# A scan and mixture-of-experts kernel: state handed over by GpSimd, C rows spread for two steps at a time, float32r weight parts used from the third tile on

## The chip, the cores and the metric

The kernel runs on one core of a Trainium2 chip. The metric is the device time of one execution in microseconds (us). The core has five engines with queues of their own that run in program order: TensorE (PE, matmul; its weight loads are shown as PEld), VectorE (DVE), ScalarE (ACT), GpSimd (POOL) and SyncE (SP, which issues the DMAs here). Semaphores order them against each other.

## The reference, cut to what matters

Per batch b (4 of them, 256 positions, width 256) a state-space layer is computed and then a feed-forward layer with two shared and eight routed experts:

```python
delta = softplus(dt_proj(dt_lo) + b);  A = -exp(A_log)          # 256 channels, 16 states
def step(state, (d_t, B_t, C_t, u_t)):
    state = state * exp(d_t[..., None] * A) + (d_t * u_t)[..., None] * B_t[:, None, :]
    return state, einsum('ben,bn->be', state, C_t)
y = (scan of step over 256 positions + D*u) * silu(z);   x = x + tanh(g0) * y
h = silu(x' @ Wg_e.T) * (x' @ Wu_e.T) for 2 shared + 8 experts (x' = layernorm(x)), FF = 176
out = x + tanh(g1) * (shared_down + 2.5 * top-2 weighted expert_down)
```

## The kernel before, in words

**Scan.** The 256 channels are two halves of 128 partitions. A *step* m takes two of the 16 states (NS = 2) over one half of the positions (128 of 256), for both channel halves: a tile of 128 x 512 in four rows of 128 columns. A batch has 16 steps: 0 to 7 of it do the first half of the positions, 8 to 15 the second, so there are 64 steps and 8 half-batches, called *tiles* (numbers 0 to 7). For a step ScalarE writes the decays exp(delta*A) into PSUM (`exps`, L642, four activations, ring psA of two); GpSimd writes delta*u*B (`times_b`, L1010, ring dbu of three); VectorE scans (L896, L902) and multiplies with C (`prod`, L913, ring of three); GpSimd adds the products of the steps of a tile (L1034; for tile 0 TensorE does, L528). C comes from TensorE, which spreads a row of C over the 128 partitions by a matmul with a 0/1 matrix `sel` (`spread_c`, L518, one step at a time, ring psC of two).

The first-half steps scan all four rows with one instruction: column 0 of each row of the decays is zero, so a row starts afresh. ScalarE keeps the last column of each row (`keep_ends`, L721, `ends`). The second-half steps need four instructions of 128 columns, each with its `ends` column as initial value (L902), and their decays have 128 columns instead of 127. Before the next batch ScalarE zeroes column 0 again (L638).

**From scan to experts.** When GpSimd has added the eight products of a tile (`prod` i on GpSimd is the addition of step i; the last ones are 15, 23, 31 ...), TensorE sums it with D*u (`y_sum`, L541, L545), VectorE gates (`gate_y`), TensorE transposes, VectorE adds the residual and the statistics, GpSimd makes the variance (`variance`, L1061 to L1067, four small operations), ScalarE normalizes, and the tile goes through ten *units* (units 10t to 10t+9): `up` on TensorE, `gate` on ScalarE (L771) and VectorE (L984), `mul` on VectorE (L807, L811). A unit with even j is two float32 matmuls (L599, each two instructions in the trace). One with odd j is six float32r matmuls (L609 to L611) on the high and low parts of weights and features (`whi`, `wlo`, `hnhi`, `hnlo`); the parts of the weights are made once, early, by ScalarE (`weights_hi`, L763) and GpSimd (`weights_lo`, L1054) from a staged copy that lies in `hcat`; unit 1 waits for all five. Four groups of a tile's hidden columns are transposed (L583), copied (`hidden`, L780) and multiplied with the down weights (`down`, L451, all 28 instructions of a tile at one place), accumulated in psD, which `y_sum`, `to_tokens`, `to_features` and `logits` use too. Then `finish` (L991) and the output DMA.

**Order.** Every engine follows a list of tasks written out by hand (`ORDER`, L88), `task:number`. A GpSimd or ScalarE task `scan:i` prepares step i+1. Start: `z_stats:0` to `z_stats:3` on VectorE need the input x (the last three batches by `d_x`), then `split0:0` to `split2:0`, `log_1:0`, `log_2:0`, `delta0:0` to `delta2:0`, and after that the first `dbu`. SP sends at the start ctx, w_x, w_dt, sel (768 KB), ident and x, then after the first projection B (broadcast), `staged` (two DMAs of 880 KB), `wup` (two of 880 KB) and `wdn`.

## Time and profile before

| what | value |
|---|---|
| median of 3 runs (lowest to highest) | 270.29 us (270.20 to 270.37) |
| the profiled execution's own time | 269.66 us |
| its span, first to last instruction | 267.7 us |
| mean granted TensorE clock (share of full) | 0.923 |
| PE busy, share of the span | 222.0 us, 83% |
| PEld busy | 167.9 us, 63% |
| DVE busy | 227.0 us, 85% |
| ACT busy | 175.5 us, 66% |
| POOL busy | 182.0 us, 68% |
| chain that ended last | PE 40%, DVE 24%, POOL 22%, issue 7%, DMA 3% |

The span is the time between the first and the last instruction that the profiler saw; the execution's own time is 1.96 us longer. Busy shares are means over stages with different limits; the profile also tells of each engine's idle time what ended it.

### The profile page before, as it was taken

The numbers are of one execution on the slowest core, as the hardware profiler recorded it, in microseconds if no ns is written. First come the engines' busy times: TensorE is split into PE (matmuls) and PEld (weight loads), VectorE is DVE, ScalarE is ACT, GpSimd is POOL, SyncE is SP. The second block draws the span as 40 slices with busy tenths as digits, with TensorE's granted clock in tenths as the row PEclk, the third lists the DMA queues.
The fourth block names the chain that finished last, engine by engine and source line by source line (L and its number), as shares of the span: only waits on it lengthen the run. The fifth ranks groups of instructions, "written<-read, shape, count | busy, mean of one in ns | idle before, by whom it ended". The sixth has DMA issues, their size and how long they took to land.

```text
span 267.7 us, 4168 instructions
## 1 busy us (share of the span) xinstructions
PE 222.0 (83%) x1093; PEld 167.9 (63%) x1093; DVE 227.0 (85%) x590; ACT 175.5 (66%) x536; POOL 182.0 (68%) x187
## 2 busy tenths in 40 slices
PE   8841983576847589999968979999999989999994
PEld 3421652354625368778746767687787778678883
DVE  1789999999999999999999998999798999563231
ACT  3579989965799695857577886584674562251121
POOL 0238999999899999998574998989586574120000
PEclk9985698559997599999999997999999999999999
DMA  6789953000025000000071000000000000000000
GB/s 175 230 269 386 364 189 157 0 0 2 0 80 240 0 1 0 22 1 0 24 271 44 1 20 2 2 0 22 0 1 21 2 0 0 20 2 1 21 0 20
DMA packets 9559, 17.34 MB, mean 65 GB/s; under 512 B 824, under 2 KB 8800, under 8 KB 8928
## 3 DMA queue, kind: packets, MB, share of 16 engines
q1 hardware_dynamic: 9248, 16.94, 18.3%
q8 instruction: 8, 0.13, 0.2%
q10 hardware_dynamic: 288, 0.16, 0.2%
q14 instruction: 15, 0.12, 0.1%
HBM read 15.97 MB, written 1.11 MB: 64 GB/s over the span
## 4 chain that ended last, share of the span: by engine, by line
PE 40%; DVE 24%; POOL 22%; issue 7%; DMA 3%; ACT 2%; SPq 1%; DVEq 0%; POOLq 0%; ACTq 0%
PE psD L451 14%; PE psU L599 11%; POOL dbu L1010 11%; DVE hs L902 7%; POOL acc L1034 5%; POOL wlo L1054 3%; PE psM L583 3%; DVE ag L984 3%; DVE prod L913 3%; PE psU L609 3%; DMA x_sb<-in_x 3%; PE psU L610 3%; PE psU L611 3%; DVE hs L896 3%; DVE hcat L811 2%
## 5 line engine op out<-in xcount | busy, mean ns | idle before, releaser
L1010 POOL TENSOR_TENSOR dbu<-du,bb 128x512 f32<-128x512 f32 x64 | 80.5, 1273 | 9.9 <-DVE du L379 4.6
L642 ACT ACTIVATE psA<-delta,aneg 128x127 f32<-128x127 f32 (+1 forms) x256 | 78.2, 357 | 6.2 <-DVE hs L902 3.4
L1034 POOL TENSOR_TENSOR acc<-acc,prod 128x512 f32<-128x512 f32 x42 | 54.2, 1291 | 16.4 <-DVE prod L913 15.0
L599 PE MATMUL psU<-wup,hnT 128*128 128x352 f32 x160 | 58.9, 493 | 1.7 <-DVE hcat L807 1.0
L771 ACT ACTIVATE tg<-psU 128x176 f32<-128x176 f32 x80 | 24.7, 315 | 48.3 <-PE psU L599 29.4
L902 DVE TENSOR_TENSOR_SCAN hs<-psA,ends,dbu 128x128 f32<-128x128 f32 x128 | 50.4, 456 | 0.2 <-DVE prod L913 0.2
L451 PE MATMUL psD<-wdn,hT 128*128 128x256 f32 x224 | 50.2, 380 | 0.0
L451 PEld LDWEIGHTS psD<-wdn,hT 128*128 128x128 f32 x224 | 42.1, 190 | 5.8 <-DVE wtok L977 0.3
L913 DVE TENSOR_TENSOR prod<-hs,psC 128x512 f32<-128x512 f32 x64 | 41.9, 673 | 0.6 <-DVE hs L896 0.4
L984 DVE SCALAR_TENSOR_TENSOR ag<-tg,psU 128x176 f32<-128x176 f32 x80 | 25.3, 327 | 17.8 <-ACT tg L771 17.5
L896 DVE TENSOR_TENSOR_SCAN hs<-psA,dbu 128x512 f32<-128x512 f32 x32 | 38.3, 1209 | 0.3 <-POOL dbu L1010 0.3
L599 PEld LDWEIGHTS psU<-wup,hnT 128*128 128x128 f32 x160 | 28.9, 199 | 13.4 <-DVE hcat L811 2.1
L609 PE MATMUL psU<-whi,hnhi 128*128 128x352 f32 x80 | 32.5, 406 | 1.4 <-DVE hcat L811 1.3
L518 PE MATMUL psC<-parts,sel 96*128 96x128 bf16 x128 | 16.7, 236 | 13.2 <-DVE prod L913 12.8
L610 PE MATMUL psU<-wlo,hnhi 128*128 128x352 f32 x80 | 26.3, 328 | 0.0
L611 PE MATMUL psU<-whi,hnlo 128*128 128x352 f32 x80 | 26.2, 327 | 0.0
L811 DVE SCALAR_TENSOR_TENSOR hcat<-psU,wtok,ag 128x176 f32<-128x176 f32 x64 | 24.4, 394 | 1.0
L518 PEld LDWEIGHTS psC<-parts,sel 96*128 96x128 bf16 x128 | 10.5, 107 | 22.7 <-DVE prod L913 15.9
L780 ACT COPY hT<-psM 128x512 f32<-128x512 f32 (+1 forms) x32 | 16.1, 502 | 13.2 <-PE psM L583 13.0
L583 PE MATMUL psM<-ident,hcat 128*128 128x128 f32 x112 | 18.0, 277 | 4.0 <-DVE hcat L811 3.8
L609 PEld LDWEIGHTS psU<-whi,hnhi 128*128 128x128 f32 x80 | 15.8, 197 | 4.8 <-DVE hcat L811 3.4
L583 PEld LDWEIGHTS psM<-ident,hcat 128*128 128x128 f32 x112 | 12.4, 140 | 8.9 <-issue 4.5
(117 smaller groups left out, 317.3 us busy)
## 6 DMA issues: line engine op xcount, KB each, us to landing
bb<-brows SPq DMA_DIRECT2D x3, 2048.0 KB, 7.1
hcat<-in_w_up SPq DMA_DIRECT2D x2, 880.0 KB, 8.9
wup<-in_w_up SPq DMA_DIRECT2D x2, 880.0 KB, 11.6
wdn<-in_w_down SPq DMA_DIRECT2D x1, 1664.0 KB, 14.1
x_sb<-in_x SPq DMA_DIRECT2D x4, 256.0 KB, 6.8
bb<-brows SPq DMA_DIRECT2D x1, 1024.0 KB, 4.7
out<-outb SPq DMA_DIRECT2D x8, 128.0 KB, 1.7
sel<-in_sel SPq DMA_DIRECT2D x1, 768.0 KB, 6.0
```

What stands on the lines that cost most here:

```text
L451: last = pe.matmul(psD[:, :], hT[0:m, g % HT_RING, c:c + P], wdn[0:m, f, :], start=(f == 0), stop=(f == FB - 1))
L583: last = pe.transpose(psM[0:m, c:c + P], hcat[:, t % 2, f * P:f * P + m], ident[:, :])
L599: last = pe.matmul(dst, hnT[:, b % 2, k, lh * P:(lh + 1) * P], wup[:, j // 2, k, :], start=(k == 0), stop=(k == KT - 1))
L609: pe.matmul(dst, h_hi, w_hi, start=(k == 0), stop=False)
L610: pe.matmul(dst, h_hi, w_lo, start=False, stop=False)
L611: last = pe.matmul(dst, h_lo, w_hi, start=False, stop=(k == KT - 1))
L642: last = act.activation(dst[:, j, h, c:], delta[:, b % 2, h, l0 + c:l1], ACT.Exp, scale=aneg[:, h * DS + s0 + j:h * DS + s0 + j + 1])
L896: dve.tensor_tensor_scan(hs[:, i % 2], psA[:, i % DA_RING], dbu[:, i % DBU_RING], 0.0, ALU.mult, ALU.add).then_inc(s_scan, 1)
L902: last = dve.tensor_tensor_scan(hs[:, i % 2, row], psA[:, i % DA_RING, row], dbu[:, i % DBU_RING, row], ends[:, i % HALF, c:c + 1], ALU.mu ...
L913: dve.tensor_tensor(tile(prod[:, i % PROD_RING]), tile(hs[:, i % 2]), c.unsqueeze(2).broadcast_to([P, NS, EH, l1 - l0]), ALU.mult).then_in ...
L1010: pool.tensor_tensor(tile(dbu[:, m % DBU_RING]), du[:, b % 2, :, l0:l1].unsqueeze(1).broadcast_to(shape), bb[:, b % 2, s0:s0 + NS, l0:l1]. ...
L1034: pool.tensor_tensor(acc[:, p % 2], before, prod[:, i % PROD_RING], ALU.add).then_inc(s_add, 1)
```

## The change

1. **Hand-over of the state.** The second half is scanned with one instruction of 512 columns too. ScalarE makes the decays of position 128 for a whole batch (`decay`, two activations of 16 columns, four times). GpSimd multiplies them with `ends`, four steps at a time (`carry`, 128 x 16, eight times), and adds the result into column 0 of the four rows of `dbu` (`fix`, 128 x 4, 32 times). VectorE's second-half scan waits for its `fix`. The zeroing copies (L638) are gone, all decays have 127 columns.
2. **C rows.** `spread_c:i` does steps 2i and 2i+1 and waits for the products up to 2i-3; ring psC is still two of 512 columns, so it holds four steps. `sel` is 96 x 32 instead of 96 x 32 x 128, and read with a step of 0.
3. **Weights.** All ten raw units lie in `wup`, loaded by two DMAs of five whole units each. Units j = 1, 5, 9 use float32r parts from tile 2 on and j = 3, 7 from tile 3 on; before that they are float32 (12 of 80 units change). `weights_lo` waits for its own unit; four are made where five were, the fifth behind step 36's dbu. `features_hi` and `features_lo` of tiles 0 and 1 go.
4. **Down.** Transposing, copying and the down product are tasks of one group each (`turn`, `hidden`, `down`, 32 of each).
5. **All lists are written anew**, SP's too (`finish:1` now behind `xproj:3 dt:3`). VectorE's begins `z_stats:0 z_stats:1 split0:0 split1:0 split2:0 z_stats:2 z_stats:3 log_1:0`; GpSimd has `z_stats:3` at the start.

`step_range`, `sum_of` and `tiles_in` also know an unhalved batch, but `HALVED` is true for all four, so the steps are those of before.

```diff
+SPLIT = ((1, 2), (3, 3), (5, 2), (7, 3), (9, 2))
+CONVERT = sorted(range(NSPLIT), key=lambda k: (SPLIT[k][1], SPLIT[k][0]))
...
     "SyncE": """
-        xproj:0 dt:0 xproj:1 dt:1 xproj:2 dt:2 finish:0 finish:1 xproj:3 dt:3 finish:2 finish:3 finish:4
+        xproj:0 dt:0 xproj:1 dt:1 xproj:2 dt:2 finish:0 xproj:3 dt:3 finish:1 finish:2 finish:3 finish:4
...
     "GpSimd": """
+        z_stats:0 z_stats:1 z_stats:2 z_stats:3 first:0 scan:0 scan:1 scan:2 scan:3 scan:4 weights_lo:0 scan:5
+        scan:6 carry:0 weights_lo:1 scan:7 scan:8 scan:9 fix:8 fix:9 fix:10 weights_lo:2 weights_lo:3 carry:1
+        scan:10 scan:11 fix:11 prod:9 fix:12 scan:12 scan:13 fix:13 fix:14 prod:10 variance:0 delta0:1 scan:14
...
-        sel = sb("sel", [P, 2 * DS, P], BF16)
+        sel = sb("sel", [P, 2 * DS], BF16)
...
-                        for k in range(KT):
-                            sp.dma_start(staged[:, :, k], w_up[:, 1::2, k]).then_inc(d_wst, 16)
-                        for k in range(KT):
-                            sp.dma_start(wup[:, :, k], w_up[:, 0::2, k]).then_inc(d_wup, 16)
+                        for k in range(2):
+                            sp.dma_start(wup[:, NU // 2 * k:NU // 2 * (k + 1)],
+                                         w_up[:, NU // 2 * k:NU // 2 * (k + 1)]).then_inc(d_wup[k], 16)
...
                     if i >= 2:
-                        pe.wait_ge(s_prod, i - 1)
-                    for j in range(NS):
-                        last = pe.matmul(psC[:, i % 2, j * P:(j + 1) * P], sel[0:XROWS, DS + s0 + j, :],
-                                         parts[:, b % 2, l0:l1], start=True, stop=True)
+                        pe.wait_ge(s_prod, 2 * i - 2)
+                    for m in (2 * i, 2 * i + 1):
+                        b, s0, ns, l0, l1 = step_range(m)
+                        for j in range(ns):
+                            c = m % 2 * L + j * (l1 - l0)
+                            last = pe.matmul(psC[:, i % 2, c:c + l1 - l0], row(DS + s0 + j),
+                                             parts[:, b % 2, l0:l1], start=True, stop=True)
...
+                    if j not in SLOT or t < SPLIT[SLOT[j]][1]:
+                        for k in range(KT):
+                            last = pe.matmul(dst, hnT[:, b % 2, k, lh * P:(lh + 1) * P], wup[:, j, k, :],
+                                             start=(k == 0), stop=(k == KT - 1))
+                    else:
+                        slot = SLOT[j]
+                        if t == SPLIT[slot][1]:
+                            pe.wait_ge(s_wlo, CONVERT.index(slot) + 1)
...
-                if m % DS in (0, 1) and m >= DS:
-                    act.copy(dst[:, :, :, 0], tile(zeros[:, 0:NS * EH])[:, :, :, 0])
-                c = 1 if l0 == 0 else 0
...
+                elif task == "decay":
+                    act.wait_ge(s_delta, i + 1)
+                    for h in range(EH):
+                        last = act.activation(dec[:, i % 2, :, h], aneg[:, h * DS:(h + 1) * DS], ACT.Exp,
+                                              scale=delta[:, i % 2, h, P:P + 1])
+                    last.then_inc(s_dec, 1)
...
-                    if l0 == 0:
-                        dve.tensor_tensor_scan(hs[:, i % 2], psA[:, i % DA_RING], dbu[:, i % DBU_RING], 0.0,
-                                               ALU.mult, ALU.add).then_inc(s_scan, 1)
-                    else:
-                        dve.wait_ge(s_ends, ends_of(i))
-                        for c in range(NS * EH):
-                            row = slice(c * P, (c + 1) * P)
-                            last = dve.tensor_tensor_scan(hs[:, i % 2, row], psA[:, i % DA_RING, row],
-                                                          dbu[:, i % DBU_RING, row], ends[:, i % HALF, c:c + 1],
-                                                          ALU.mult, ALU.add)
-                        last.then_inc(s_scan, 1)
+                    if second_half(i):
+                        dve.wait_ge(s_fix, ends_of(i))
+                    dve.tensor_tensor_scan(hs[:, i % 2], psA[:, i % DA_RING], dbu[:, i % DBU_RING], 0.0,
+                                           ALU.mult, ALU.add).then_inc(s_scan, 1)
...
+                elif task == "carry":
+                    b, j = divmod(i, 2)
+                    k0, k1 = j * HALF // 2, (j + 1) * HALF // 2
+                    pool.wait_ge(s_ends, HALF * b + k1)
+                    pool.wait_ge(s_dec, b + 1)
...
+                elif task == "fix":
+                    heads = dbu[:, i % DBU_RING].rearrange("p (c l) -> p c l", l=P)[:, :, 0]
+                    pool.wait_ge(s_dbu, i + 1)
+                    pool.wait_ge(s_carry, 2 * (i // DS) + (1 if i % HALF < HALF // 2 else 2))
+                    pool.tensor_tensor(heads, heads, carry[:, i % HALF], ALU.add).then_inc(s_fix, 1)
```

## Rows read from the trace of the kernel before

**Rows 1.** Busy time by stretch: PE, PEld, DVE, ACT, POOL, PEclk, DMA share, GB/s
```profile
55.00:90.00 35.00, 22.90 (x105) 16.29 (x104) 34.24 (x89) 27.57 (x96) 33.44 (x31) 0.84 0.16 62
90.00:114.50 24.50, 23.52 (x119) 18.24 (x120) 23.85 (x67) 17.74 (x53) 23.75 (x24) 0.94 0.02 6
114.50:146.60 32.10, 29.10 (x156) 23.02 (x156) 31.64 (x79) 22.63 (x76) 22.68 (x25) 1.00 0.19 71
146.60:227.90 81.30, 77.90 (x404) 61.54 (x403) 75.28 (x203) 51.86 (x167) 62.25 (x60) 0.98 0.02 6
227.90:265.00 37.10, 35.66 (x179) 28.41 (x177) 15.14 (x51) 10.76 (x31) 2.10 (x6) 1.00 0.02 8
```

**Rows 2.** Timeline, start: start us, us, engine, line, op, shapes, count [idle before]
```profile
11.69 0.41 ACT L682 CAST parts<-xdbl 96x256 bf16<-96x256 f32 x1
...
12.15 0.75 DVE L921 BATCH_NORM_STATS2 zst<-x_sb 128x6 f32<-128x256 f32 x2 [1.19 <-DMA x_sb<-in_x]
...
13.10 0.72 DVE L921 BATCH_NORM_STATS2 zst<-x_sb 128x6 f32<-128x256 f32 x2
...
14.65 0.58 ACT L699 ACTIVATE psC<-psC 128x512 f32<-128x512 f32 x1
...
16.17 0.67 DVE L875 TENSOR_SCALAR dy<-psC 128x512 f32<-128x512 f32 x1
```

**Rows 3.** Groups by line on DVE: count, busy us, mean ns, idle before
```profile
L902 DVE TENSOR_TENSOR_SCAN hs<-psA,ends,dbu 128x128 f32<-128x128 f32 x128 | 50.4, 456 | 0.2 <-DVE prod L913 0.2
...
L896 DVE TENSOR_TENSOR_SCAN hs<-psA,dbu 128x512 f32<-128x512 f32 x32 | 38.3, 1209 | 0.3 <-POOL dbu L1010 0.3
```

**Rows 4.** Groups by line on POOL
```profile
L1010 POOL TENSOR_TENSOR dbu<-du,bb 128x512 f32<-128x512 f32 x64 | 80.5, 1273 | 9.9 <-DVE du L379 4.6 <-DVE hs L902 3.4 <-DVE hs L896 1.7
...
L1050 POOL TENSOR_TENSOR hnlo<-hnT,hnhi 128x256 fp32r<-128x256 f32 x8 | 5.8, 728 | 3.4 <-ACT hnhi L759 3.4
...
L1044 POOL TENSOR_TENSOR znh<-zmv,zrs 128x2 f32<-128x2 f32 x4 | 0.8, 193 | 0.3
```

**Rows 5.** Timeline of POOL, from the first dbu to step 31's addition
```profile
21.17 7.48 POOL L1010 TENSOR_TENSOR dbu<-du,bb 128x512 f32<-128x512 f32 x6 [4.61 <-DVE du L379]
...
36.80 1.68 POOL L1054 TENSOR_TENSOR wlo<-hcat,whi 128x704 fp32r<-128x704 f32 x1
...
48.42 0.23 POOL L1061 TENSOR_SCALAR ve<-mv 128x1 f32<-128x1 f32 x1
48.73 0.58 POOL L1063 TENSOR_TENSOR rs<-ve,minus_half 128x1 f32<-128x1 f32 x1
...
49.88 1.26 POOL L368 TENSOR_TENSOR dnc<-drel,dnc 128x512 f32<-128x512 f32 x1
...
111.80 2.69 POOL L1034 TENSOR_TENSOR acc<-acc,prod 128x512 f32<-128x512 f32 x2
```

**Rows 6.** Timeline of PE: one unit of each kind, and a float32 unit early
```profile
55.58 2.69 PE L599 MATMUL psU<-wup,hnT 128*128 128x352 f32 x4
...
235.05 1.35 PE L599 MATMUL psU<-wup,hnT 128*128 128x352 f32 x4
236.23 0.38 PE L561 MATMUL psD<-ident,hn 128*128 128x128 f32 x2
236.42 0.43 PE L609 MATMUL psU<-whi,hnhi 128*128 128x352 f32 x1
...
237.48 0.51 PE L571 MATMUL psD<-wg,hnT 128*128 128x8 f32 x4
```

**Rows 7.** Groups by line: the C rows' weight loads
```profile
L518 PEld LDWEIGHTS psC<-parts,sel 96*128 96x128 bf16 x128 | 10.5, 107 | 22.7 <-DVE prod L913 15.9 <-issue 3.3 <-DVE dnc L882 0.5
```

**Rows 8.** Timeline, the end: last transposes on PE, last operation on DVE
```profile
261.98 0.41 PE L583 MATMUL psM<-ident,hcat 128*128 128x128 f32 x2 [0.87 <-DVE hcat L811]
...
265.03 0.48 DVE L991 SCALAR_TENSOR_TENSOR outb<-psD,gates,x_sb 128x256 f32<-128x256 f32 x1 [3.19 <-PE psD L451]
```

More of the change, by code:

```diff
@@ L113 @@
+        turn:26 up:72 up:73 down:25 up:74 up:75 turn:27 down:26 down:27 turn:28 up:76 up:77 turn:29 up:78 up:79
+        down:28 turn:30 down:29 turn:31 down:30 down:31
     """,
@@ L140 @@
-        hidden:67 gate:67 norm:7 gate:68 to_features_out:7 features_hi:7 gate:69 logits_out:7 hidden:70 gate:70
-        gate:71 gate:72 gate:73 hidden:71 hidden:74 gate:74 gate:75 gate:76 gate:77 hidden:77 gate:78 gate:79
-        flush:80 flush:81
+        z_norm:0 spread_b:1 first:0 scan:0 tanh_u:1 keep_ends:0 scan:1 scan:2 weights_hi:0 keep_ends:1
+        keep_ends:2 scan:3 xproj_out:1 keep_ends:3 scan:4 decay:0 weights_hi:1 keep_ends:4 scan:5 scan:6
+        keep_ends:5 weights_hi:2 weights_hi:3 keep_ends:6 keep_ends:7 z_gate:0 scan:7 scan:8 dt_out:1 soft_exp:1
@@ L171 @@
-        prod:62 mul:60 scan:63 gate:61 mul:61 prod:63 finish:5 gate:62 gate:63 mul:62 mul:63 gate_y:7 gate:64
+        load:0 tap0:0 tap1:0 tap2:0 silu_u:0 z_stats:0 z_stats:1 split0:0 split1:0 split2:0 z_stats:2 z_stats:3
+        log_1:0 log_2:0 delta0:0 delta1:0 tap0:1 delta2:0 tap1:1 tap2:1 scan:0 scan:1 prod:0 silu_u:1 scan:2
+        prod:1 prod:2 scan:3 scan:4 prod:3 split0:1 scan:5 prod:4 prod:5 split1:1 scan:6 scan:7 prod:6 prod:7
+        split2:1 z_gate:0 scan:8 scan:9 prod:8 gate_y:0 prod:9 residual:0 log_1:1 stats:0 scan:10 scan:11
@@ new lines @@
+        z_gate:2 prod:37 gate:22 gate:23 mul:22 mul:23 split0:3 scan:38 scan:39 split1:3 prod:38 prod:39 gate:24
+        gate:25 mul:24 mul:25 split2:3 finish:1 scan:40 gate:26 scan:41 mul:26 gate:27 prod:40 mul:27 scan:42
+        route:3 prod:41 gate:28 gate:29 mul:28 mul:29 prod:42 gate_y:4 scan:43 residual:4 log_1:3 scan:44
+        gate:30 prod:43 gate:31 log_2:3 stats:4 mul:30 mul:31 variance:4 prod:44 scan:45 prod:45 scan:46 gate:32
+        prod:46 mul:32 gate:33 mul:33 finish:2 scan:47 prod:47 gate:34 gate:35 mul:34 mul:35 route:4 gate:36
@@ L174 @@
-        mul:74 mul:75 gate:76 mul:76 gate:77 gate:78 mul:77 mul:78 gate:79 mul:79 finish:7
+        mul:69 route:7 gate:70 gate:71 mul:70 mul:71 gate:72 gate:73 mul:72 mul:73 gate:74 gate:75 mul:74 mul:75
+        finish:6 gate:76 mul:76 gate:77 mul:77 gate:78 gate:79 mul:78 mul:79 finish:7
     """,
     "GpSimd": """
-        z_stats:0 z_stats:1 z_stats:2 first:0 scan:0 scan:1 scan:2 scan:3 scan:4 weights_lo:0 weights_lo:1
-        scan:5 scan:6 scan:7 scan:8 weights_lo:2 scan:9 weights_lo:3 weights_lo:4 scan:10 scan:11 scan:12 prod:9
@@ new lines @@
+        scan:19 scan:20 prod:18 scan:21 prod:19 carry:2 prod:20 scan:22 scan:23 prod:21 fix:24 scan:24 scan:25
+        scan:26 fix:25 fix:26 fix:27 prod:22 variance:1 prod:23 prod:25 carry:3 scan:27 fix:28 scan:28 scan:29
+        delta0:2 scan:30 fix:29 fix:30 prod:26 fix:31 prod:27 delta1:2 prod:28 delta2:2 prod:29 scan:31 scan:32
+        prod:30 prod:31 variance:2 scan:33 scan:34 scan:35 weights_lo:4 features_lo:2 prod:33 scan:36 prod:34
+        scan:37 scan:38 variance:3 carry:4 prod:35 prod:36 scan:39 scan:40 scan:41 carry:5 fix:40 fix:41 fix:42
@@ L190 @@
+        features_lo:6 fix:61 fix:62 fix:63 prod:59 prod:60 prod:61 prod:62 prod:63 variance:7 features_lo:7
     """,
@@ L459, in spread_b @@
                 for i in range(4):
-                    last = pe.matmul(psU[:, k, i * P:(i + 1) * P], sel[0:XROWS, 4 * k + i, :], parts[:, 0, 0:P],
+                    last = pe.matmul(psU[:, k, i * P:(i + 1) * P], row(4 * k + i), parts[:, 0, 0:P],
                                      start=True, stop=True)
@@ L616, in _ @@
                 elif task == "down":
-                    for g in range(NG * i, NG * (i + 1)):
-                        down(g)
+                    down(i)
         @block.scalar
```

403 lines of the change are left out of this document (202 added, 201 removed).

## The prediction

> **What bounds the kernel now.** I read first how busy each engine is in four stretches that end at events of the scan [rows 1]. From 55 to 90 us VectorE is busy 34.2 of 35 and GpSimd 33.4 of 35, while TensorE has 22.9 and a granted clock of 0.84: these stretches go at the pace of the scan, and on the scan's path GpSimd has hardly a gap. From 114.5 on TensorE is busy 29.1 of 32.1, 77.9 of 81.3 and 35.7 of 37.1 us, with VectorE close behind (31.6 and 75.3) and GpSimd with 28.5 us to spare. So there are two parts. Until about 114.5 us, when GpSimd has added step 31 (the row that starts at 111.80 and lasts 2.69 ends at 114.49 [rows 5]), GpSimd sets the pace; from there TensorE does, and loses 3.0 + 3.4 + 1.4 = 7.8 us to gaps, most of them made by a full VectorE.
>
> The forecast is therefore: when does step 31's addition end, and how much work and how many gaps has TensorE after it?
>
> **Start.** VectorE waits 1.19 us for x, in `z_stats:1`, and does three more of these pairs ahead of the splits; the exponential that `log_1:0` needs has ended at 14.65 + 0.58 = 15.23, but `log_1:0` starts at 16.17 [rows 2]. The 768 KB of sel stood ahead of x in SP's queue and are now 6 KB, so x comes earlier; and only two `z_stats` stand ahead of the splits, whose input is there at 12.10 [rows 2]. Counted on: the first two pairs, each 0.95 (12.15 to 13.10 [rows 2]), are over by 12.1, three splits of 0.4 end at 13.35, two more pairs at 15.25. `log_1:0` then starts at 15.25, 0.9 us earlier, and so does everything down to the first dbu: 21.17 becomes 20.25 [rows 5]. If SP's queue gives nothing back the gain is 0; the exponential allows no more than 0.94.
>
> **The scan on VectorE.** The 128 instructions of 128 columns take 50.4 us, 1.58 a step; the 32 of 512 columns take 38.3, 1.20 a step [rows 3]. One instead of four saves 0.38 x 32 = 12.1 us of VectorE, half of it before 114.5. Where GpSimd sets the pace this is worth nothing in itself; what is late next there is GpSimd's own queue.
>
> **GpSimd up to step 31's addition.** Its list is counted with 1.24 for a dbu or an addition (7.44 for six, with the seventh right behind [rows 4, 5]), 1.66 for a `weights_lo`, 1.46 for a `variance` (48.42 to 49.88), 0.7 for a `features_lo` [rows 4, 5]. Before, from the first dbu: 90.9 us, which with 21.17 gives 112.1; it ended at 114.5, so 2.4 us were gaps. In the new list one dbu, one `weights_lo`, one `variance` and two `features_lo` fewer stand ahead of that addition (-1.24 - 1.66 - 1.46 - 1.4 = -5.8) and 16 `fix` and 4 `carry` more. No row shows such an operation. The nearest is 128 x 2 at 193 ns [rows 4], the longest small one 128 x 1 at 0.58 (a power [rows 5]); with the step from one small operation to the next (0.31, from 48.42 to 48.73) I take 0.25, since the two-input product is the same kind. That is 20 x 0.25 = 5.0; at the ends 3.9 and 11.6. Sum: 90.9 - 5.8 + 5.0 = 90.1. With gaps of 2.0 (VectorE is quicker, but a `carry` waits for ScalarE's `ends` and holds up every dbu behind it) step 31 is added at 20.25 + 90.1 + 2.0 = 112.35, 2.1 us earlier than before.
>
> [...]
>
> On the way tiles 0 and 1 come later, not earlier: up to step 15's addition the new list has 2.6 us more, so the first units start some 1.5 us later. That is covered, since TensorE is busy only 22.9 of 35 us there [rows 1].
>
> **TensorE after that.** A float32 unit takes 1.18 us (235.05 to 236.23), a float32r one 1.06 (236.42 to 237.48) [rows 6]. From `y_sum:3` on the new list has 34 float32 and 28 float32r units where 30 and 31 were: +1.54. It also has one normalized tile's transposes and logits more (+0.7), one group of transposes more (+0.44), one projection (-0.86) and two steps' C rows (-0.44) fewer. The sum is +1.4; the work was 29.1 + 77.9 + 35.7 = 142.7 [rows 1] and becomes 144.1. The other converted units lie in tiles 0 and 1, where float32 at the low clock costs up to 2.69 [rows 6]; their cover is TensorE's 12.1 idle us of 55 to 90, and without it ten of them would cost 10 x (2.69 - 1.06) = 16 us.
>
> The gaps were 7.8. One of 0.87 goes at the end: TensorE waited there for the last product before the last transposes [rows 8], and the new list has `down:29` between. The others come from VectorE, whose list from product 31 to product 63 was 113.5 us in 118 and is now 104.8, so it has 13 us to spare instead of 4. `down` in groups of 1.7 us instead of 6 lets `gate` and `mul` follow the units, but psD, which `to_features` and `y_sum` need too, is held longer from `down` to `finish`. I take 5 us of gaps; the ends are 1 (all covered) and 8 (nothing gained).
>
> **Edits at nothing.** C rows: the same number of matmuls. A weight load takes 107 ns [rows 7]; a read with step 0 could make it dearer, but the loads lie beside the matmuls, and products now find C up to four steps ahead. If all 128 doubled they would be 13.7 us of loads more, spread over the whole scan, about half of it in the part where TensorE has gaps. `decay`: eight small activations on ScalarE against six small copies fewer, on an engine busy 27.6 of 35 and later 51.9 of 81.3 us [rows 1]. The weights' two DMAs carry the bytes of the four; only `weights_hi:1` needs the second of them early, and ScalarE's decays are queued behind that wait: 0 to 1 us, inside the 2.0 of gaps. On SP's list `finish:1` now stands behind `dt:3`, which waits for step 31's dbu; only `finish:3` needs its buffer. Nothing. GpSimd's fifth `weights_lo` stands ahead of `features_lo:2`, which `up:21` waits for: by the sum it ends near 119, when TensorE gets there too; up to 1 us, inside the 5.
>
> **Sum.** 112.35 + 144.1 + 5.0 = 261.4 for the last down product, where it was 265.03 [rows 8]; the last operation and the output take 2.7 as before: span 264.1. With the 1.96 around it the profiled execution would take 266.1 against 269.66, that is 3.6 less. The median was 0.63 above the profiled one, so I forecast 266.7 (rounded from 270.29 - 3.6). A measurement tells 0.2%, 0.54 us, from no change.
>
> **Rivals.**
> *Everything is filled.* No gap up to step 31 (-2) and 1 instead of 5 after it (-4): 260.7. For it: VectorE's 12.1 us and the finer `down`. Against: TensorE's gaps are also hand-backs through ScalarE and psD, which stay.
> *The heads cost GpSimd more.* The path in a second half is now `keep_ends` on ScalarE, `carry`, `fix`, scan, and `fix` stands in a queue that is full until 114.5. At 0.58 each (the longest small row) the 20 operations are 6.6 us more, and 266.7 becomes 273.3. The point from which it decides is 3.6 / 20 = 0.18 above my 0.25, that is 0.43 per operation or the same in waits behind a `carry`. For it: GpSimd has no slack there. Against: the 193 ns.
> *Low clock.* Tiles 0 and 1 have only float32 units; if TensorE stays at 1.2 GHz there (the clock was 0.84 of 2.4 GHz from 55 to 90, after stretches with few matmuls), ten converted units take up to 16 us more, and with 12.1 us of cover 4 to 5 come out: 271.5. Against: they are at the low level only if the neighbours leave gaps.
> *The order gives it back.* VectorE's saving lies off the path in the first half, and psD held longer costs in the second what VectorE gives: 270.5. This is also the case that the change does not do what it says: shorter scans, same end.
>
> **How the numbers follow.** The forecast has 0.60 (263.5 to 269.8), everything filled 0.12, dear heads 0.16, low clock 0.06, given back 0.06. Faster: 0.58 + 0.12 = 0.70; same: 0.02 + 0.02 + 0.02 = 0.06; slower: 0.14 + 0.06 + 0.04 = 0.24. The range reaches from the filled case, 261.0, to the dear heads, 273.0; about half of each of these two lies outside, and a little of the low clock.
>
> **What would show it.** First dbu near 20.3. The second-half scans in 32 instructions of 1.2 us. `fix` and `carry` at 0.19 to 0.3 us, few waits of VectorE for them. Step 31's addition ends near 112.4; if it ends at 116 or later the heads or the waits behind `carry` are dearer. After it TensorE busy for 144 us with about 5 idle. L518's weight loads still 107 ns. If VectorE is still full after 114 us, or TensorE waits for psD's readers, the forecast fails there.

## The result, and the profile after

The changed kernel took 259.61 us (median; 257.9 to 261.05), the kernel before 270.25 beside it: ratio 0.961, 95% interval 0.955 to 0.968. That is 10.6 us less where 3.6 were forecast, and below the range of 261.0 to 273.0. In a later comparison it took 257.53 us (257.41 to 257.94), ratio 0.953 (0.950 to 0.955); the profiled executions of the two have spans of 256.1 and 255.8 us. Executions that lie more than 1.5% above the fastest of their kernel are left out of the ratios, but not out of the medians and ranges given here. Because medians of one kernel can lie 2 us apart, I read effects of a few microseconds from the profiled executions, one for each run: the span, and **T3**, the start of the first matmul of `y_sum:3` that reads `acc` (it follows step 31's addition at once). The last operation, `finish:7`, starts when the last down product is there.

| profiled execution | before | after |
|---|---|---|
| time / span | 269.66 / 267.7 | 257.9 / 256.1 |
| first dbu | 21.17 | 20.89 |
| T3 | 114.86 | 110.39 |
| `finish:7` | 265.03 | 253.43 |
| from T3 to `finish:7` | 150.2 | 143.0 |

So 4.5 us were gained until T3 and 7.1 after it. How far can such stretches be trusted? The changed kernel was profiled twice (the second time as after_again): from the first dbu to T3 both took 89.50 us, from T3 to `finish:7` 143.04 and 143.00, and runs whose edit does not reach a stretch stay within 0.2 us of that. The kernel before is less steady: the run `start`, whose edits are the small `sel` and the order of the first tasks, took 95.1 and 149.4 us for the two stretches where the kernel before took 93.7 and 150.2. So half a microsecond can be read against the changed kernel, but only 1 to 1.5 us against the one before.

T3 in the changed kernel and, for later, in the run no_handover (timelines):

```profile
110.39 1.11 PE L586 MATMUL psD<-acc,ident 128*128 128x256 f32 x4
```

```profile
116.56 1.03 PE L579 MATMUL psD<-acc,ident 128*128 128x256 f32 x4
```

Busy time by stretch, after (the columns of [rows 1]; the last three rows end within 1 us of the same events as there):

```profile
55.00:90.00 35.00, 28.63 (x120) 18.79 (x120) 34.11 (x71) 29.15 (x92) 34.66 (x37) 0.93 0.15 61
110.30:142.00 31.70, 29.72 (x151) 22.58 (x150) 31.12 (x79) 26.47 (x91) 30.57 (x40) 1.00 0.19 72
142.00:216.50 74.50, 73.26 (x399) 60.55 (x398) 68.07 (x160) 49.53 (x161) 59.30 (x69) 1.00 0.02 7
216.50:254.00 37.50, 36.89 (x188) 30.28 (x186) 15.66 (x52) 10.72 (x31) 2.71 (x6) 1.00 0.02 8
```

After T3 TensorE is busy 139.9 us, with 3.2 us of gaps: 2.0 and 1.2 in the first two stretches and none that counts in the last, where before there were 7.8. From 55 to 90 us it is busy 28.6 instead of 22.9 us, at a clock of 0.93 instead of 0.84 [rows 1]. The low clock feared for the first two tiles came only at their start: the granted clock was 0.50, its 1.2 GHz level, from 55 to 60 us with TensorE busy all 5.0 of it, and 1.00 from 60 to 90. VectorE and GpSimd were full there too (4.8 and 5.0 of these 5 us).

The start of the changed kernel (timeline), to set beside [rows 2] and the first row of [rows 5]:

```profile
15.25 0.58 ACT L735 ACTIVATE psC<-psC 128x512 f32<-128x512 f32 x1
15.86 0.69 DVE L918 TENSOR_SCALAR dy<-psC 128x512 f32<-128x512 f32 x1
```

`log_1:0` follows the exponential at once, as forecast; but the exponential itself ends at 15.83, not at 15.23, since the first projection was read 0.6 us later. Of the 0.9 us counted on, 0.3 are left.

VectorE's and GpSimd's groups by line, to set beside [rows 3] and [rows 4]:

```profile
L940 DVE TENSOR_TENSOR_SCAN hs<-psA,dbu 128x512 f32<-128x512 f32 x64 | 76.7, 1212 | 2.9 <-ACT psA L678 2.0 <-POOL dbu L1072 0.5 <-DVE prod L949 0.4
```

```profile
L1072 POOL TENSOR_TENSOR dbu<-dbu,carry 128x4 f32<-128x4 f32 x32 | 6.2, 216 | 0.2
```

VectorE's scans take 76.7 us instead of 88.7. A `fix` takes 0.19 us of GpSimd (6.2 / 32), a `carry` 0.22 (eight are 1.8); VectorE waits 0.5 us in all for a `fix`.

The end of GpSimd's path, and of the kernel (timelines; before: the last row of [rows 5], and [rows 8]):

```profile
107.64 2.67 POOL L1086 TENSOR_TENSOR acc<-acc,prod 128x512 f32<-128x512 f32 x2
```

```profile
250.42 0.38 PE L624 MATMUL psM<-ident,hcat 128*128 128x128 f32 x2
...
253.43 0.48 DVE L1027 SCALAR_TENSOR_TENSOR outb<-psD,gates,x_sb 128x256 f32<-128x256 f32 x1 [5.40 <-PE psD L490]
```

Step 31's addition ends at 110.31. The 0.87 us in front of the last transposes are gone, as forecast.

### The profile page after: what moved, and what is told of

Read it like the earlier page. It is cut to its first block, busy times and chain, and to the rows that moved or that the text cites. A ratio compares the mean times of both kernels' runs of the same rounds, so it can differ in the third digit from the quotient of the medians.

```text
span 256.1 us, 4103 instructions
## 1 busy us (share of the span) xinstructions
PE 217.0 (85%) x1069; PEld 162.6 (63%) x1069; DVE 214.6 (84%) x494; ACT 175.6 (69%) x536; POOL 186.7 (73%) x225
## 4 chain that ended last, share of the span: by engine, by line
PE 45%; POOL 27%; issue 15%; DVE 8%; ACT 4%; POOLq 0%; DVEq 0%
PE psD L490 13%; PE psU L641 12%; POOL acc L1086 11%; POOL dbu L1046 10%; PE psU L652 3%; PE psM L624 3%; PE psU L654 3%; PE psU L653 3%; POOL wlo L1107 2%; DVE hs L940 2%; PE psD L586 1%; POOL dbu L1072 1%; PE psC L506 1%; ACT psA L678 1%; DVE xh L889 1%
## 5 line engine op out<-in xcount | busy, mean ns | idle before, releaser
L678 ACT ACTIVATE psA<-delta,aneg 128x127 f32<-128x127 f32 x256 | 78.0, 357 | 2.1 <-DVE hs L940 1.6
L940 DVE TENSOR_TENSOR_SCAN hs<-psA,dbu 128x512 f32<-128x512 f32 x64 | 76.7, 1212 | 2.9 <-ACT psA L678 2.0
L641 PE MATMUL psU<-wup,hnT 128*128 128x352 f32 x208 | 72.6, 479 | 3.6 <-DVE hcat L854 2.8
L490 PE MATMUL psD<-wdn,hT 128*128 128x256 f32 x224 | 52.0, 381 | 0.9 <-issue 0.9
L641 PEld LDWEIGHTS psU<-wup,hnT 128*128 128x128 f32 x208 | 38.1, 195 | 20.3 <-DVE hcat L854 4.2
L490 PEld LDWEIGHTS psD<-wdn,hT 128*128 128x128 f32 x224 | 41.4, 190 | 6.9 <-issue 1.3
L652 PE MATMUL psU<-whi,hnhi 128*128 128x352 f32 x56 | 23.0, 410 | 0.0
L624 PE MATMUL psM<-ident,hcat 128*128 128x128 f32 x112 | 17.7, 275 | 3.9 <-ACT hT L825 3.1
L559 PE MATMUL psC<-parts,sel 96*128 96x128 bf16 x128 | 12.3, 225 | 7.3 <-DVE prod L949 5.6
L654 PE MATMUL psU<-whi,hnlo 128*128 128x352 f32 x56 | 18.0, 322 | 0.0
L653 PE MATMUL psU<-wlo,hnhi 128*128 128x352 f32 x56 | 18.0, 322 | 0.0
L530 PE MATMUL psM<-u,wx 128*104 128x256 f32 x16 | 5.2, 455 | 8.5 <-DVE u L898 8.5
L889 DVE SCALAR_TENSOR_TENSOR xh<-psM,cwh,xh 128x253 f32<-128x253 f32 (+2 forms) x24 | 10.0, 473 | 2.2 <-ACT xh L699 2.2
```

The costliest lines, as they stand in the source:

```text
L490: last = pe.matmul(psD[:, :], hT[0:m, g % HT_RING, c:c + P], wdn[0:m, f, :], start=(f == 0), stop=(f == FB - 1))
L624: last = pe.transpose(psM[0:m, c:c + P], hcat[:, t % 2, f * P:f * P + m], ident[:, :])
L641: last = pe.matmul(dst, hnT[:, b % 2, k, lh * P:(lh + 1) * P], wup[:, j, k, :], start=(k == 0), stop=(k == KT - 1))
L652: pe.matmul(dst, h_hi, w_hi, start=(k == 0), stop=False)
L653: pe.matmul(dst, h_hi, w_lo, start=False, stop=False)
L654: last = pe.matmul(dst, h_lo, w_hi, start=False, stop=(k == KT - 1))
```

## Experiments

Theory A was the prediction's: GpSimd sets the pace until T3, TensorE after it. Theory B: VectorE's shorter scans are themselves the gain. Theory D: until T3 VectorE and GpSimd are both full, and both set the pace. It came up after scan4, handover, allf32 and down_together. Theories C, E, F and W are named where they are tested. Each kernel was timed beside the kernel before on the same chip; "ratio" is against that one.

### The hand-over, and the scan

**scan4**, the changed kernel with four scans again, start value 0:

```
-dve.tensor_tensor_scan(hs[:, i % 2], psA[..], dbu[..], 0.0, ..)
+for c in range(NS * EH):     # second halves
+    dve.tensor_tensor_scan(hs[:, i % 2, cols], psA[.., cols], dbu[.., cols], 0.0, ..)
```

> The changed kernel, except that each second-half scan is again four instructions of 128 columns (each starts from 0 and the heads stay added by GpSimd, so only VectorE's time changes): VectorE has 12 us more to do, GpSimd, ScalarE and TensorE nothing. Theory A (GpSimd sets the pace until step 31's addition, TensorE after it): VectorE has some 7 us idle in the 106 us after 110.3 and some before, so of the 12 us only a part comes out: 260.5 to 263.5, step 31's addition later by 0 to 1.5 us. Theory B (the shorter scans are the gain, VectorE is what the kernel waits for): the 12 us come back nearly whole, 268 to 272.

260.42 us (259.75 to 263.77), ratio 0.962 (0.956 to 0.967); span 259.2, T3 112.95. It doesn't test what it should: VectorE got only 4.5 us more (43.0 + 38.2 against 76.7), because a scan from a constant takes 402 ns where one from a value in memory takes 456. Even so the span is 3.1 us longer, and T3 2.6 us later where theory A allowed 1.5. The medians (260.42 against 259.61) would not show this.

**scan_old**, the same with the start value read from memory (multiplied by a zero in psA, so the result is the same), and **scan_old_first**, the same in the first two sequences only:

```
-    .., dbu[.., cols], 0.0, ..)
+    .., dbu[.., cols], minus_half[:, 0:1], ..)       # all; or only where i < 32
```

> The changed kernel with the four scans of 128 columns and a start value read from memory in every second half (the value is multiplied by a zero, the heads stay as they are): VectorE gets back the whole 12.1 us of the kernel before (4 x 456 ns against 1212), all else the same. The run with start value 0 cost only 4.7 us of VectorE and 0.8 in time. Theory A (GpSimd alone sets the pace until step 31's addition): 261 to 264. Theory D (VectorE is as full as GpSimd until then, both 97% busy from 20 to 110 us; what either gets more comes out): the 6 us before step 31's addition come out nearly whole and 0 to 3 of those after it, 265 to 269.

> The same only in the first two sequences (16 steps, VectorE 6.1 us more, all of it before step 31's addition). Theory A: 260 to 262. Theory D: 264 to 266, step 31's addition near 115.

scan_old: 266.79 us (266.45 to 267.12), ratio 0.985 (0.981 to 0.989); span 265.3, T3 117.20. scan_old_first: 264.75 us (264.02 to 265.06), ratio 0.977 (0.972 to 0.982); span 263.1, T3 117.39. The 6.1 us of VectorE before T3 make T3 7.0 us later, the whole of it; the 6.1 after it make 2.2 of span. Theory A falls, D's forecast (264 to 266 for the second run, 265 to 269 for the first) holds; that GpSimd paces too is for the next two runs.

**pool_early** and **pool_late**, three more small additions behind each `fix`, before and after T3:

```
 pool.tensor_tensor(heads, heads, carry[:, i % HALF], ALU.add).then_inc(s_fix, 1)
+if i < 32:                                     # pool_late: i >= 32
+    for q in range(3):
+        pool.tensor_tensor(spare[q], carry[:, i % HALF], carry[:, i % HALF], ALU.add)
```

> The changed kernel with three more small additions of GpSimd behind each fix of the first two sequences (16 x 3 = 48 operations on 128 x 4, results not used, 0.15 to 0.22 us each, 7 to 10 us). Theories A and D: GpSimd has 2 us to spare in the 90 before step 31's addition, so that comes 5 to 9 us later and the time is 264 to 269. Theory B (only VectorE paces there; taking 6.6 us off GpSimd brought that addition 0.8 earlier): 260 to 262.5.

> The same 48 additions in the last two sequences, after step 31's addition. Theories A and D: TensorE sets the pace there, GpSimd has 5 us idle from 140 to 180 and 13 from 180 to 220: 259.5 to 262. If GpSimd's chain of fix, scan and product were still on the path, 265 to 268.

pool_early: 264.32 us (264.06 to 264.73), ratio 0.976 (0.973 to 0.980); span 262.5, T3 116.71. pool_late: 260.77 us (259.91 to 261.7), ratio 0.963 (0.958 to 0.968); span 258.1, T3 110.49. The 48 operations are 8.0 us of GpSimd; before T3 they cost 6.3 of T3 and 6.4 of span, after it 2.0. So before T3 more work on GpSimd comes out nearly whole, as more work on VectorE does. The trace shows both, as the busy time from 21 to 110 us (columns as in [rows 1]) of the kernel before, after, scan_old_first and pool_early:

```profile
21.00:110.00 89.00, 60.69 (x275) 44.63 (x276) 87.60 (x203) 74.66 (x227) 86.29 (x78) 0.81 0.28 103
```

```profile
21.00:110.00 89.00, 62.11 (x271) 41.58 (x272) 86.35 (x164) 76.05 (x229) 87.63 (x93) 0.88 0.27 106
```

```profile
21.00:110.00 89.00, 60.21 (x243) 40.84 (x244) 86.06 (x197) 74.05 (x220) 82.32 (x89) 0.81 0.28 106
```

```profile
21.00:110.00 89.00, 60.33 (x254) 39.96 (x254) 81.77 (x152) 73.50 (x219) 88.12 (x136) 0.84 0.27 104
```

Before, VectorE was the fuller of the two (87.6 of 89). After, both are full. With the old scans in the first two sequences GpSimd falls to 82.3 and waits for VectorE; with GpSimd's extra operations VectorE falls to 81.8.

**no_handover**, the changed kernel without decay, carry and fix:

```
-"GpSimd": .. carry:0 .. fix:8 fix:9 ..      "ScalarE": .. decay:0 ..
-dve.wait_ge(s_fix, ends_of(i)); one scan of 512 columns
+dve.wait_ge(s_ends, ends_of(i)); four scans of 128, start value ends[:, i % HALF, c:c + 1]
```

> The changed kernel without the hand-over: no decay, carry and fix; a second half scans in four instructions from the kept ends and its decays fill all 128 columns, as in the kernel before; orders, C rows, units and downs stay. VectorE has 12.1 us more, GpSimd 8.0 less (4.2 of it before step 31's addition). The old scan alone, with GpSimd's additions kept, gave a span 9.2 us longer. Theory D (both engines full until step 31's addition, VectorE the tighter): GpSimd's 8 us give back 0 to 2, 264 to 267. Rival (GpSimd's small operations are what costs, the hand-over is worth little in sum): 260 to 263.

267.27 us (265.58 to 267.51), ratio 0.987 (0.982 to 0.992); span 265.5, T3 116.56, `finish:7` at 262.78. As long as scan_old, though GpSimd has 8 us less to do: in the new order the hand-over is worth 9.4 us of span (265.5 against 256.1), and GpSimd's part in it costs nothing that shows in the span as long as VectorE is the late one. From 21 to 110 us:

```profile
21.00:110.00 89.00, 61.66 (x245) 41.69 (x246) 86.17 (x198) 73.07 (x218) 79.39 (x69) 0.81 0.27 104
```

Without the hand-over the new lists leave GpSimd nearly 10 of 89 us to spare, and VectorE alone is full. The hand-over takes work from VectorE and spends some of that spare time, until both are full. This run splits the change:

| | T3 | T3 to `finish:7` |
|---|---|---|
| before | 114.86 | 150.2 |
| all but the hand-over | 116.56 (+1.7) | 146.2 (-4.0) |
| after | 110.39 (-6.2) | 143.0 (-3.2) |

The differences of the last row, the hand-over's, are well clear of the spread. Those of the row above it are not in full: `start`, with nearly the lists of before, has T3 at 116.05 and 149.4 us behind it. Against it the +1.7 shrinks to 0.5 and the -4.0 to 3.2.

**handover**, the kernel before with the hand-over alone, its lists otherwise as they were; and **handover_busy**, the same with the C rows of the first 32 steps issued three times:

```
+"GpSimd": .. scan:7 carry:0 fix:8 .. scan:10 carry:1 fix:11 ..    "ScalarE": .. scan:4 decay:0 ..
+pool.tensor_tensor(heads, heads, carry[:, i % HALF], ALU.add); one scan of 512 columns behind it
 for j in range(NS):                            # handover_busy: three times, for i < 32
     pe.matmul(psC[:, i % 2, j * P:(j + 1) * P], ..)
```

> The kernel before with the hand-over alone: decay on ScalarE, carry and fix on GpSimd, one scan of 512 columns in a second half; orders, C rows, units and downs as before. Theory A: step 31's addition comes 1 to 4 us later (20 small operations of 0.15 to 0.22 in a full queue), after it VectorE's 6 us take 2 to 4 out of TensorE's gaps of 7.8: 268 to 272, about no change. Theory B: VectorE's 12 us come out, 260 to 263, the whole of the measured gain.

> The kernel before with the hand-over alone (275.4), and each C row of the first 32 steps issued three times, so that TensorE is busy some 7 us more until step 31. In the run without it TensorE's granted clock was 0.50 from 55 to 75 us and VectorE and ScalarE waited for its units. Theory W (the low clock in tiles 0 and 1 is what made the hand-over alone slower): the clock from 55 to 90 rises over 0.8 from 0.65, step 31's addition comes at 114 to 119 instead of 125, 268 to 272. Rival (the old lists, planned for the long scans, make the waits): clock or not, 274 to 279.

handover: 275.37 us (274.17 to 278.59), ratio 1.016 (1.010 to 1.023); T3 125.14. handover_busy: 275.07 us (273.31 to 277.28), ratio 1.018 (1.011 to 1.025); T3 121.69. The same edit that is worth 9.4 us in the new order costs 4 to 5 in the old one. All of that lies before T3: from the first dbu to T3 the two take 101.8 and 100.6 us where the kernel before takes 93.7, and from T3 to `finish:7` 148.7 and 148.8 where it takes 150.2. The profiled execution of handover is the slowest of its four (278.59), so its trace is read with care. From 55 to 75 us, first handover, then handover_busy:

```profile
55.00:75.00 20.00, 14.28 (x43) 10.06 (x44) 14.61 (x35) 11.30 (x36) 18.85 (x18) 0.50 0.00 0
```

```profile
55.00:75.00 20.00, 14.81 (x69) 11.15 (x70) 16.03 (x38) 11.66 (x40) 18.91 (x18) 0.78 0.01 1
```

The clock was 0.50 (all of it at 1.2 GHz) in one and 0.78 in the other, and the times of the two kernels are the same. Of the 3.45 us that T3 came earlier, 2.2 are the start (first dbu at 21.10 instead of 23.31, where x had come late). So what the higher clock brought is at most 1.2 us; the kernel before had 0.90 in these 20 us, which neither run reaches, so a part of the low clock's cost may be left in both. GpSimd is nearly full here (18.9 of 20) and VectorE is not; over 21 to 110 us neither is in handover (79.8 and 77.3 of 89). The old lists had GpSimd's work laid out for a scan that leaves it room. That the order as such is the rest of the cause is what remains, not what a run isolates.

### Weights

**allf32**, all 80 units float32, and **more_f32r**, two more units as parts from tile 4 on:

```
-if j not in SLOT or t < SPLIT[SLOT[j]][1]:
+if True:                                     # allf32; weights and features tasks leave the lists
-SPLIT = ((1, 2), (3, 3), (5, 2), (7, 3), (9, 2))
+SPLIT = ((1, 2), (3, 3), (4, 4), (5, 2), (6, 4), (7, 3), (9, 2))        # more_f32r
```

> The changed kernel with all 80 units in float32, no high and low parts: GpSimd has four subtractions of weights (6.6 us) fewer before step 31's addition and one and six of features after it, ScalarE 11 copies fewer, TensorE 28 x 0.12 = 3.4 us more after that addition. Theory A: the addition comes up to 6.6 us earlier, less where VectorE (little idle there) is late next, and TensorE takes 3.4 back: 255.5 to 259.5, the addition at 104 to 108. Theory B: GpSimd's time is worth nothing, 259.6 to 263.

> The changed kernel with two more units (4 and 6) as float32r parts from tile 4 on: 8 units of 1.06 instead of 1.18 us on TensorE after step 31's addition (the run with all 28 in float32 was 3.3 us slower, 0.12 each), two copies on ScalarE and two subtractions of 1.68 on GpSimd more between step 31 and step 45. Theory (TensorE sets the pace there, GpSimd has room): 0.5 to 1 us less than the changed kernel of this call. Rival (GpSimd is 28.9 of 30 us busy from 110 to 140): no gain, or 1 to 3 us more.

allf32: 262.96 us (262.19 to 264.56), ratio 0.973 (0.967 to 0.978); span 260.4, T3 109.59. Here A missed: 6.6 us less of GpSimd moved T3 by 0.8, and even that is the start, since the first dbu came at 20.14 instead of 20.89. From there to T3 it took 89.45 us against 89.50: nothing gained. GpSimd falls to 81.3 of the 89 us, and VectorE is as full as before:

```profile
21.00:110.00 89.00, 65.08 (x274) 43.97 (x275) 86.11 (x165) 72.92 (x224) 81.34 (x91) 0.85 0.26 102
```

The other side is TensorE's: from T3 to `finish:7` it is busy 145.1 instead of 139.8 us, 5.3 us for 28 units, so a float32 unit costs 0.19 more than a float32r one and not the 0.12 that I read from one pair [rows 6]. Span: 4.3 us longer. more_f32r: 258.45 us (258.14 to 261.51), ratio 0.959 (0.953 to 0.965); span 256.3, T3 110.05: no gain beside 257.53. (To make room, its warm-up matmuls at the very start are 448 columns wide instead of 512.) Step 39's sum came 0.5 us later than in after_again (141.28 against 140.73), GpSimd being 28.9 of 30 us busy from 110 to 140; what TensorE saved was waited away.

### Down, C rows, start

**down_together**, the changed kernel with the four groups where the last one stood; **together_later**, the same with `finish` three or four instructions later on VectorE; **down_split**, the kernel before with its groups spread out:

```
-down:4 down:5 up:24 up:25 down:6 down:7       -down:0 spread_c:30 spread_c:31 up:14 up:15 spread_c:32
+up:24 up:25 down:4 down:5 down:6 down:7       +down:0 spread_c:30 spread_c:31 up:14 down:1 up:15 down:2 ..
-finish:4 scan:59 gate:52 gate:53 mul:52       (together_later)
+scan:59 gate:52 gate:53 mul:52 finish:4
```

> The changed kernel with the four groups of down products of a tile issued together, where the last group stood; all else the same. Theory A: TensorE's work is the same, but the 5 to 6 us in which no unit is issued make VectorE and ScalarE wait and their return late: gaps 1 to 4 us more, 260.5 to 264. Rival C (the finer downs cost nothing and give nothing, the 4.6 us fewer of TensorE gaps came from VectorE's shorter list): within 0.5 us of the changed kernel.

> The run with the four groups of down products together (282.55), with finish moved back on VectorE by three or four instructions for tiles 0 to 5. In that run VectorE stood 20.8 us in front of finish. Theory F (what a whole tile's down products cost is VectorE's wait in finish, with scans and gates queued behind it): 268 to 275, VectorE's wait for psD down to 5 to 12 us. Rival (what costs is that TensorE issues no unit for 6 us, or psD is held): 280 to 284.

> The kernel before with the down products of tiles 0 to 6 in four groups, each behind a unit, where all four stood together (no group crosses another user of psD). Theory E (the finer down products are what fills TensorE's gaps after step 31; together they cost the changed kernel 23 us): gaps of 7.8 become 4 to 6, 266 to 269. Rival (the gain of the finer downs exists only in an order planned for them): 269.5 to 273.

down_together: 282.55 us (282.13 to 283.93), ratio 1.045 (1.040 to 1.050). together_later: 290.57 us (290.18 to 291.87), ratio 1.076 (1.072 to 1.079). down_split: 298.77 us (294.55 to 300.76), against 270.62 for the kernel before; no ratio is on record for it. All three are far outside what any theory gave. VectorE's waits (for what: us in total, times, longest), first in down_together, then in together_later, then in the changed kernel:

```profile
DVE outb L1024 <- PE psD L487: 33.9, 8, 7.7
DVE ag L1017 <- ACT tg L815: 13.7, 17, 1.6
```

```profile
DVE ag L1017 <- ACT tg L815: 29.9, 23, 4.5
DVE outb L1024 <- PE psD L487: 15.8, 3, 7.7
```

```profile
DVE ag L1020 <- ACT tg L818: 14.7, 17, 2.8
DVE outb L1027 <- PE psD L490: 9.2, 5, 5.4
```

In down_together VectorE stands in front of `finish` for 33.9 us instead of 9.2 (some 21 of them for the first six tiles), with scans, products and gates behind it. Moving `finish` back halves that wait, doubles the one for ScalarE's `tanh`, and makes TensorE wait for `finish` (4.0 and 3.0 us, where down_together has 0.4):

```profile
PE psD L601 <- DVE outb L1024: 4.0, 4, 1.5
PE psD L578 <- DVE outb L1024: 3.0, 2, 1.5
```

So theory F names the wait rightly, but moving `finish` is not its cure: the time grew by 8 us where 7 to 15 less were expected. psD is one buffer for `down`, `y_sum`, `to_tokens`, `to_features` and `logits`, and its places in two in-order lists depend on each other: moving TensorE's alone cost 23 to 28 us in either kernel, and moving VectorE's three or four places back as well cost 8 more. What the finer groups are worth in an order made for them is not isolated by these runs.

**c_twice_late** and **c_twice_early**, each C row's matmul issued twice in blocks 18 to 31, or 0 to 17:

```
-for j in range(ns):
+for j in [j for _ in range(2 if i >= 18 else 1) for j in range(ns)]:      # c_twice_early: i < 18
```

> The changed kernel with each block of four C-row matmuls issued twice in the last blocks (18 to 31, after step 31's addition): 56 matmuls more. By the 5.1 us that the 56 show as their busy time it costs TensorE 3.6 to 5.1 us, and as TensorE is busy 139.9 of the 143.1 us there, the time is 262.5 to 265. If TensorE were not what sets the pace there, 259.6 to 261.

> The same for the blocks 0 to 17, before step 31's addition: 72 matmuls more. TensorE has 17 us idle from 20 to 55 and 6 from 55 to 90 there; VectorE and GpSimd are full: 259.5 to 261.5. If TensorE's path to VectorE's products counts, 262 to 265.

c_twice_late: 259.32 us (259.18 to 261.26), ratio 0.960 (0.954 to 0.965); span 257.4, T3 110.28. From T3 on TensorE is busy 141.9 instead of 139.8 us, psC's share 8.27 instead of 5.13: 56 more matmuls are 3.1 us (my 3.6 to 5.1 took the first matmul's latency in a block for its price). 1.4 us of it come out (144.4 from T3 to `finish:7` instead of 143.0); the rest went into gaps and beside other matmuls. The time is below even the range for the case that TensorE is not what sets the pace, which starts at the 259.6 of the first comparison. That is a weak confirmation that TensorE sets the pace after T3. c_twice_early: 257.94 us (257.68 to 258.23), ratio 0.953 (0.948 to 0.957); span 255.9, T3 110.16: 72 matmuls more before T3 cost nothing.

**after_again** and **warm_again**, the changed kernel and c_twice_early once more, side by side:

> The changed kernel once more, beside the run with the early C rows issued twice, whose four times (257.7 to 258.2) lay at the lower end of this one's (257.9 to 261.05). If those are two draws of the same, both come out at 258 to 260 with the ranges overlapping; the first dbu and step 31's addition tell where a slower execution loses its time (20.9 and 110.3 in the one profiled).

> The changed kernel with the C rows of the first 18 blocks issued twice, as before. Theory W (TensorE, busier from 20 to 110 us, stays at 2.4 GHz more often, so that tiles 0 and 1 are never late): 257.7 to 258.5 again, 1 us or more below the changed kernel of this call, with a narrow spread. Rival (chance, the start varies): the same median within 0.5 us.

257.53 us (257.41 to 257.94) and 257.92 (257.61 to 257.99), ratios 0.953 (0.950 to 0.955) and 0.954 (0.951 to 0.956). Theory W falls: the early matmuls bring nothing, and the changed kernel's first four times simply lay higher. Why they did stays open.

**start**, the kernel before with the small sel and the new places of `z_stats` alone:

```
-sel = sb("sel", [P, 2 * DS, P], BF16)         -z_stats:2 z_stats:3 split0:0 split1:0 split2:0
+sel = sb("sel", [P, 2 * DS], BF16)            +split0:0 split1:0 split2:0 z_stats:2 z_stats:3
```

> The kernel before with the start alone: sel as 6 KB read with step 0, and two z_stats ahead of the splits and two behind. In the two traces so far log_1:0 started at 16.17 (before) and 15.86 (after, where it followed the exponential directly); in the run with the hand-over alone, with the old start, x came late and the first dbu at 23.31. Theory: first dbu between 20.2 and 20.9 instead of 21.17, in time 0.3 to 0.9 us less and a narrower spread of the runs: 269 to 270.3. Rival (the single column of weights costs TensorE): L518's matmuls or weight loads grow, 271 or more.

270.29 us (268.44 to 273.57), ratio 0.998 (0.995 to 1.001): no difference that counts, and the spread of the runs is no narrower. First dbu at 20.94, 0.23 earlier. Step 31's addition ends 1.2 us later than in the kernel before (115.69 against 114.49), which none of its edits explains; it is the spread named above. The single column read with step 0 costs nothing that shows.

## Why the prediction was wrong

The sign was right, but the size was a third of the true one, and what the forecast says of the scan on VectorE was wrong. The last down product was forecast for 261.4 and came at 253.4, 8.0 us sooner: 2.0 until T3 (112.35 forecast, 110.39), 4.3 of TensorE's work after it (144.1 forecast, 139.8) and 1.7 of its gaps. By its steps:

**Start.** The reorder works, the 0.9 us became 0.3, since the first projection was 0.6 us later in that execution. In after_again the first dbu is at 20.63. A small miss.

**The scan on VectorE: this step failed.** "One instead of four saves 12.1 us" is right (12.0). "Where GpSimd sets the pace this is worth nothing in itself" is wrong. [rows 1] had VectorE busy 34.2 of 35, 23.85 of 24.5 us before 114.5, more than GpSimd in both; I read GpSimd as the pace and VectorE as beside it. Two engines that hand each step to each other were both full, and both paced. scan_old_first puts 7.0 us on T3 for the scans of the first two sequences, no_handover 6.2 on T3 and 3.2 after it. So the hand-over, which the forecast booked as a cost of 5.0 us at T3, was a gain of 6.2 there.

**GpSimd's list.** Counted 90.1 and 2.0 of gaps; measured 89.4 from first dbu to the addition's end, gaps included. The small operations were 16 x 0.19 + 4 x 0.22 = 3.9 instead of 5.0, and GpSimd's idle time up to that addition went from 2.7 (90.6 busy of 93.3) to 1.4 us (88.1 of 89.4). T3 came out 2.0 us from the forecast, and that was luck, as the count of one full engine says nothing of the other. Two errors cancelled: the 5.8 us taken off GpSimd's list were booked as a gain, though allf32 shows that taking another 6.6 off it gains nothing, and the hand-over was booked as a cost. By the same counting no_handover, which lacks the 5.0, would have had its T3 at 20.5 + 85.1 + 2.0 = 107.6, and it came at 116.56. The row of 193 ns was the right one to take, with `fix` at 0.19 us. Small operations are not free there: in pool_early 48 of 0.17 us cost 6.4 us. Dear heads (273.3) needed 0.43 each and did not come.

**TensorE after T3: the term of 144.1 + 5.0 was 6.1 too high.** This is the larger part of the miss in size. TensorE's work by the tile written, from 114.5 to 265.0 us before and from 110.3 to 254.0 after:

| us busy | before | after | forecast change | measured |
|---|---|---|---|---|
| units (psU) | 78.3 | 76.6 | +1.5 | -1.6 |
| C rows (psC) | 7.2 | 5.1 | -0.4 | -2.1 |
| down, sums, transposes (psD) | 58.2 | 60.1 | +0.7 | +1.9 |
| turns, projections (psM) | 17.7 | 17.0 | -0.4 | -0.7 |

The sum, with what overlaps, went from 142.7 to 139.9 instead of to 144.1. By what allf32 shows (0.19 more for a float32 unit) the units should even have cost more than I counted, yet their time fell. Three things were missed. A dip of the clock in the kernel before is gone; it stands in these two rows (columns as in [rows 1]) and cost some 1.4 us (half of 2, and a fifth of 2, of a TensorE that was busy throughout):

```profile
162.00:164.00 2.00, 2.00 (x6) 1.47 (x5) 1.76 (x13) 1.02 (x4) 1.92 (x2) 0.50 0.00 0
164.00:166.00 2.00, 2.00 (x11) 1.58 (x11) 1.05 (x4) 0.90 (x3) 1.55 (x3) 0.79 0.00 0
```

[rows 1] shows it as 0.98 in 81.3 us, which I passed over. `start`, which has the lists of before and no such dip, confirms the size: its units take 76.9 us instead of 78.3, and TensorE's sum is 141.5 instead of 142.7. So of the two traces with these lists only one has the dip, and it is not counted as a gain of the change. "C rows: the same number of matmuls" was right and the price was not: after T3 60 matmuls in blocks of two take 7.2 us and 56 in blocks of four take 5.1. With the 0.056 us that a further matmul adds (c_twice_late), a block costs an estimated 0.13 to 0.14 us beyond its matmuls, and there are 14 blocks instead of 30. The same works the other way for `down`: 28 blocks instead of 7 cost some 1.3 us more (L451's 44.0 to L490's 45.3 for the same 196 matmuls), which I had not counted. With the dip's 1.4 taken off, the units took 0.3 us less than before where 1.5 more were forecast, so some 2 us are left; that units of the kernel before start more often behind a wait, and so cost more, is argued and not shown.

**Gaps.** 3.2 instead of 5.0, inside the 1 to 8 given. VectorE's relief is in it: without the hand-over T3 to `finish:7` is 3.2 us longer. VectorE was still full until 142 us (31.1 of 31.7), which the forecast had named as a sign of failing, and TensorE's gaps were small all the same.

**Edits at nothing.** The step-0 read cost nothing that shows (start). No run isolates `decay`, the two DMAs and `finish:1`; VectorE waits only 0.5 us in all for a `fix`, and `decay` lies ahead of that. `weights_lo:4` and `features_lo:2` were over at 117.9 instead of near 119, before `up:21` started at 118.6, and caused no gap.

**The rivals.** Everything filled (260.7) came closest, and not by its mechanism: the gaps were 3.2 and not 1. Given back, low clock and dear heads did not occur. But the order is no small matter: the hand-over alone in the old lists is 4 to 5 us slower than before, and that is where the slower outcome was hidden. The nearest that I had named was "the order gives it back", with 0.06, for other reasons and for the new lists.

What stays open: the units' 2 us; how the other edits' gain after T3 (-4.0 us, of which `start` leaves 3.2) divides between C rows, weights and the places of `down`; and whether their +1.7 before T3 is real.

## What to carry to other kernels

Where two engines pass each step to each other and both are over 96% busy, as here, each of them sets the pace: work taken from one is worth only what the other has to spare (6.6 us off GpSimd gained nothing), and work added to either comes out nearly whole (7.0 for 6.1 us, 6.3 for 8.0). Price an edit on every engine that is as full as the one you took for the bound, and check it by adding a known amount to each in turn. An instruction list written for one set of durations is part of the edit: the same hand-over was worth 9.4 us in lists made for it and cost 4 to 5 in the old ones.

## What the runs showed of the hardware

- A scan of 128 columns takes 402 ns when it starts from a constant and 456 to 461 ns when it starts from a value in memory; four of them in a row 1.34 and 1.58 us, one of 512 columns 1.21.
- Small operations of GpSimd on 128 x 4 have a duration of 202 ns but take 0.17 us each when three follow one another (8.0 us for 48, pool_early).
- A bf16 matmul of 128 columns behind others adds 0.056 us at the full clock (3.1 us for 56, c_twice_late), where the median duration of the group after T3 is 219 ns.
- Issuing C rows twice did not raise the granted clock from 20 to 55 us (0.72 in c_twice_early, 0.74 and 0.65 in the two traces of the changed kernel). Between 55 and 75 us it was 0.78 in handover_busy, with the C rows three times, and 0.50 in handover: one execution each, so that the matmuls raised it is not shown.
